# Even and odd batches as two streams half a round apart in a twelve-layer attention kernel

## The reference

```
x (8, 256, 128), cond (8, 128), context (8, 1601, 96)
 0 self  attention, 16 heads of 64, rotary     6 self  attention, 16 heads of 64
 1 cross attention, 16 heads of 64, rotary     7 cross attention, 16 heads of 64
 2 feed-forward (gelu)                         8 feed-forward (gated gelu)
 3 self  attention, 16 heads of 8              9 self  attention, 16 heads of 8, q and k normed
 4 cross attention, 16 heads of 8             10 cross attention, 16 heads of 8
 5 feed-forward (tanh gelu)                   11 feed-forward (gated silu)
attention: softmax(q k^T * dh^-0.5) v, projected; cross: the 1601 context rows are keys and values
```

## Time and profile before

| what | value |
|---|---|
| time, three runs | 6185.82, 6196.47 (median), 6211.56 us |
| profiled execution | 6242.82 us, of which the span of its instructions is 6241.0 us |
| mean granted TensorE clock in it | 0.898 of 2.4 GHz |
| busy: PE, DVE, ACT, POOL | 5692.5, 4360.4, 3383.1, 2505.9 us |
| PE's weight loads | 3349.0 us |
| DMA queue of the program | 124.68 MB, 8.5% of 16 engines' span |

### The profile page before, as it was taken

One profiled execution on the slowest core, in us unless ns is written; L12 is line 12 of the kernel. 1 busy time (PEld: TensorE's weight loads), 2 busy tenths in 40 slices (PEclk: granted clock), 3 DMA queues, 4 the chain that ended last, 5 costly groups with the idle time before them and its releaser, 6 DMA issues. The chain is left out here.

```text
span 6241.0 us, 170025 instructions
## 1 busy us (share of the span) xinstructions
PE 5692.5 (91%) x66584; PEld 3349.0 (54%) x66584; DVE 4360.4 (70%) x8986; ACT 3383.1 (54%) x7674; POOL 2505.9 (40%) x2223
## 2 busy tenths in 40 slices
PE   6999899988899989998889998999888998899988
PEld 4566346643556635664356653566435665356633
DVE  6886666656788666665788867666668886666664
ACT  3455565546544556554644556555564555655555
POOL 2566016730256501673026640277103663037700
PEclk9999699987899969998899987999779998699976
DMA  4000010000100001000010000100001000010000
GB/s 111 23 16 17 13 30 16 13 20 12 44 23 16 15 15 32 14 14 18 16 44 22 16 18 12 32 13 15 19 17 45 13 16 17 11 36 13 7 17 8
DMA packets 277771, 135.56 MB, mean 22 GB/s; under 512 B 151005, under 2 KB 266301, under 8 KB 276862
## 3 DMA queue, kind: packets, MB, share of 16 engines
q1 hardware_dynamic: 276990, 124.68, 8.5%
HBM read 101.90 MB, written 3.01 MB: 17 GB/s over the span
## 5 line engine op out<-in xcount | busy, mean ns | idle before, releaser
L2266 DVE TENSOR_REDUCE max_part<-ring 128x1 f32<-128x400 f32 (+2 forms) x4608 | 2418.6, 578 | 776.1 <-PE ring L1425 768.0
L1918 ACT ACTIVATE probs<-ring 128x512 f32<-128x512 f32 (+1 forms) x4096 | 2101.2, 572 | 1337.9 <-PE ring L1425 1312.4
L1401 POOL TENSOR_TENSOR weight_sum<-weight_sum,probs 128x512 f32<-128x512 f32 (+1 forms) x1408 | 1793.7, 1274 | 150.3 <-ACT probs L1918 11.5
L1425 PE MATMUL o_acc<-probs,region 128*32 128x256 f32 (+2 forms) x13312 | 1503.1, 441 | 47.2 <-ACT probs L1918 41.4
L1425 PEld LDWEIGHTS o_acc<-probs,region 128*32 128x32 f32 (+2 forms) x13312 | 617.2, 133 | 573.8 <-issue 262.4
L1401 POOL TENSOR_TENSOR weight_sum<-probs 128x512 f32<-128x512 f32 x256 | 332.1, 1297 | 1467.7 <-PE ring L1425 923.6
L1425 PE MATMUL ring<-qop,region 64*128 64x256 f16 x9984 | 833.1, 270 | 22.6 <-ACT shift_q L1763 16.7
L1763 ACT ACTIVATE region<-ring 65x128 f32<-65x128 f32 (+4 forms) x1232 | 560.9, 474 | 413.8 <-PE ring L1425 319.8
L1425 PE MATMUL ring<-nk,nq 32*128 32x400 f16 (+2 forms) x2560 | 601.9, 401 | 65.2 <-ACT probs L1918 51.1
L1425 PEld LDWEIGHTS ring<-qop,region 64*128 64x128 f16 x9984 | 522.2, 95 | 188.2 <-issue 92.1
L1425 PE MATMUL ring<-shift_q,shift_k 64*128 64x256 f16 (+1 forms) x3840 | 618.3, 270 | 0.0
(11 more groups left out here) (181 smaller groups left out, 6668.6 us busy)
## 6 DMA issues: line engine op xcount, KB each, us to landing
stage<-in_wide SPq DMA_DIRECT2D x448, 64.0 KB, 1.9
nk<-region SPq DMA_DIRECT2D x768, 25.0 KB
wo_stage<-in_wide SPq DMA_DIRECT2D x32, 512.0 KB, 4.0
stage<-in_wide SPq DMA_DIRECT2D x64, 128.0 KB, 2.5
v_stage<-in_wide SPq DMA_DIRECT2D x128, 64.0 KB, 1.9
ff_w<-in_ff_w SPq DMA_DIRECT2D x24, 256.0 KB, 3.3
stage<-kv_split SPq DMA_DIRECT2D x64, 96.0 KB, 2.1
v_stage<-kv_split SPq DMA_DIRECT2D x128, 48.0 KB, 1.7
```

The costliest lines, as they stand in the source:

```text
L1401: pool.tensor_tensor(total, before, probs[0:rows_, (un.chunk + k) % PROBS, :], ALU.add)\
L1425: return pe.matmul(out, lhs, rhs, start=start, stop=stop, skip_group_check=True)
L1918: act.activation(to, src, ACT.Exp, scale=t.scale).then_inc(exp_done.sem, 1)
L2266: dve.tensor_reduce(dst, src, AX.X, ALU.max).then_inc(*release(one))
```

## The change

- **Two streams.** `make_items` writes a new order. A *phase* has the self and cross attention of one kind of one stream and those of the other kind of the other stream: while the even batch is in its wide pair (0, 1 or 6, 7), the odd batch is in a narrow pair (9, 10 or 3, 4), and the other way round. There are 16 steps a stream and the odd stream runs one step behind, so there are 17 phases, the first without narrow and the last without wide units. In a phase come the narrow prelude, 8 wide self units, the prelude of the wide cross attention, 4 narrow self units, the prelude of the narrow cross attention, and then the cross units of both in the order `XXxXxXXxXx+XX` (X a wide, x a narrow one, + the prelude for what the narrow stream does next).
- **Buffers** go by the number of the unit in its own kind; maxima have four slots, two for each kind; narrow units have an output tile `attn_n` of their own; the narrow values (one set instead of two) and keys leave `region`, and the column of ones in the narrow values is set once at the start by POOL and not for each batch. `NK_SLOTS` goes from 3 to 2, `RING` from 4 to 5.
- **Rotary products.** The sine product goes to an SBUF buffer `raw_sin` as an instruction that can be ordered by itself, and its bank is free then; the add takes two SBUF operands and writes `raw`; ACT's high half reads `raw`, and so does DVE's low half. The number of instructions is the same.
- **Order of jobs.** A wide cross unit makes its keys first and its q last, so that keys need no tokens. All maxima follow. The transposed context moves to the prelude of sublayer 0, and its normed form to the start of the prelude of sublayer 1.
- **Weights.** The feed-forward weights are loaded ahead of each batch's layer and no longer once for two batches.
- In `Plan`, maxima of wide and narrow units are two queues instead of one. A maximum is still one product into one bank and one reduction.

```diff
-POOL_BANKS, RING, SLOTS, PROBS = 7, 4, 4, 8
+POOL_BANKS, RING, SLOTS, PROBS = 7, 5, 4, 8
-NK_SLOTS, VS_SLOTS = 3, 4
+NK_SLOTS, VS_SLOTS = 2, 4
...
-        out = op(0) + op(1) + [("low", 0, 0)] + op(2) + [("low", 1, 0)]
-        out += op(3) + [("low", 2, 0)] + maxima(0) + op(4) + [("low", 3, 0)] + maxima(1)
-        out += vals[0:1] + [("low", 4, 0)] + maxima(2) + vals[1:2] + maxima(3)
+        out = op(1) + op(2) + [("low", 1, 0)] + op(3) + [("low", 2, 0)] + vals[0:1]
+        out += op(4) + [("low", 3, 0)] + op(0) + [("low", 4, 0), ("low", 0, 0)]
+        out += maxima(0) + maxima(1) + vals[1:2] + maxima(2) + maxima(3)
...
+STAGES = ((0, 1), (3, 4), (6, 7), (9, 10))
+SHARED = "XXxXxXXxXx+XX"
+def make_items():
+    out = [("pre", 0, 0)]
+    steps = len(STAGES) * B // 2
...
+    for phase in range(steps + 1):
+        wide = narrow = None
+        for side in range(2):
+            i = phase - side
+            if 0 <= i < steps:
+                u, k = 2 * (i // len(STAGES)) + side, i % len(STAGES)
+                if k % 2:
+                    narrow = u, *STAGES[k], k
+                else:
+                    wide = u, *STAGES[k]
+        if narrow:
+            out.append(("pre", narrow[1], narrow[0]))
+        if wide:
+            for p in range(ATT[wide[1]].units):
+                unit(wide[1], wide[0], p)
+            out.append(("pre", wide[2], wide[0]))
+        if narrow:
+            for p in range(ATT[narrow[1]].units):
+                unit(narrow[1], narrow[0], p)
+            out.append(("pre", narrow[2], narrow[0]))
+        at = {"X": 0, "x": 0}
+        for what in SHARED:
+            if what == "X" and wide:
+                unit(wide[2], wide[0], at[what])
+            elif what == "x" and narrow:
+                unit(narrow[2], narrow[0], at[what])
...
     def low_parts(un, i):
...
+                    if t.rope:
+                        dve.tensor_tensor(operand(un, i, 1)[0], raw[:, raw_slot(un, i), 0:w], high, ALU.subtract)\
+                            .then_inc(rope_low.sem, 1)
+                        return
...
+                    if one[0] == "sin":
+                        dve.wait_ge(*full(made))
...
+                        dve.tensor_tensor(raw_sin[:, 0:w], v, rope_sin[:, a0:a0 + w], ALU.mult)\
+                            .then_inc(*release(made))
+                        return
...
-                    dve.tensor_tensor(v, v, rope_sin[:, a0:a0 + w], ALU.mult).then_inc(rope_step.sem, 1)
-                    dve.wait_ge(*taken(("job", n, j - 1)))
-                    dve.wait_ge(rope_step.sem, rope_step.at(n, 3 * i + 1))
-                    dve.tensor_tensor(v, v, products, ALU.add).then_inc(rope_step.sem, 2)
+                    for product in latest([("job", n, j - 1), made]):
+                        dve.wait_ge(*taken(product))
+                    dve.tensor_tensor(turned, turned, raw_sin[:, 0:w], ALU.add).then_inc(rope_step.sem, 1)
...
-            self.part("PE", "max", due, one, 0.1 if t.cross else 0.16, deps, 0.25)
+            self.part("PE", "wide max", due, one, 0.1 if t.cross else 0.16, deps, 0.25)
...
+            self.part("PE", "narrow max", due, one, 0.1 if t.cross else 0.16, deps, 0.25)
...
-                        if kind == "ffout" and u % 2 and (s, u) != (END, B - 1):
+                        if kind == "ffout" and (s, u) != (END, B - 1):
...
-                            load_hidden_weights((FFN[s - 1] + 1) % len(FFN))
+                            load_hidden_weights(next(hidden_at))
```

More of the change, by code:

```diff
@@ L169, in make_units @@
+ITEMS = make_items()
 def make_units():
     out, chunk, wide_at, narrow_at = [], 0, 0, 0
[L171 to L178, removed]
+    for kind, s, u, *rest in ITEMS:
+        if kind == "unit":
+            t = ATT[s]
+            out.append(Unit(len(out), t, u, *rest, chunk, wide_at, narrow_at))
+            chunk += t.chunks
+            wide_at += t.wide
+            narrow_at += not t.wide
@@ L179, in make_units @@
     return out
 UNITS = make_units()
+WIDES = [un for un in UNITS if un.t.wide]
+NARROWS = [un for un in UNITS if not un.t.wide]
+FIRST_UNIT = {(un.t.sub, un.u): un for un in UNITS if un.p == 0}
 LAST_UNIT = {(un.t.sub, un.u): un for un in UNITS if un.p == un.t.units - 1}
[L186 to L195, removed]
@@ L330, in make_order @@
         put(2.0 + 6.0 * i, "split", i)
-    clock, host = 0.0, free
-    for un in UNITS:
-        t, n = un.t, un.n
[L334 to L340, removed]
+    clock, units = 0.0, iter(UNITS)
+    for what, s, u, *_ in ITEMS:
+        if what == "pre":
+            place_prelude(s, u, clock if out else free)
+            continue
+        un = next(units)
+        t, n = un.t, un.n
+        if un.p == 0 and n:
+            clock = max(clock, begins[s, u] + (12.0 if t.wide else 14.0))
         for pair in range(t.pairs):
@@ L375, in holds @@
     kind, i, k = t.jobs[j]
-    if kind == "op" and not (t.rope and k == 0):
+    if kind == "op" and t.rope:
+        return "DVE", one if k == 0 else ("sin", one[1], j)
+    if kind == "op":
         return "DVE", ("job", one[1], t.jobs.index(("low", i, 0)))
@@ L500, in pre @@
             deps = [("POOL", ("scale", old.n))] if before.wide else [("ACT", here(m - 1))]
-            if before.wide and self.wide.index(old) >= 8:
+            if before.wide and self.wo:
                 deps.append(("SP", self.wo))
@@ L551, in wide_job @@
         if kind == "op":
-            deps = self.inputs(un) if j == 0 else []
+            deps = (self.context(un) if t.cross and i else self.tokens(un)) if k == 0 else []
             if j == 0 and at >= 2:
@@ L575, in wide_job @@
             old = [("PE", ("job", self.wide[at - 1].n, self.wide[at - 1].t.shift_job))] if at else []
[L576 removed]
+            self.part("DVE", "shift", due, one, 0.15, maxima + self.turned(un))
             self.part("ACT", "cols", due, ("cols", n), 0.2, [("DVE", one), *old])
@@ L614, in narrow_job @@
         old = self.narrow[un.narrow_at - 1] if un.narrow_at else None
-        self.part("DVE", "shift", due, one, 0.15, [*maxima, ("ACT", ("cols", n - 2))])
+        self.part("DVE", "shift", due, one, 0.15, maxima + self.turned(un))
         self.part("ACT", "cols", due, ("cols", n), 0.2,
```

345 lines of the change are left out of this document (192 added, 153 removed).

## The result

The changed kernel takes 6241.3 us (median of five runs, 6235.2 to 6257.5) against 6193.1 for the kernel before: ratio 1.008, 95% interval 1.0057 to 1.0103. It is slower by 0.8%, where 8% faster was forecast.

A forecast was written before the change was run, and what follows sets the result against it. Bound before the change: PE in wide cross attentions, DVE in sublayer 0, neither in narrow ones. A phases 2660, B phases 2536, phase 0 346 and the last phase 180 sum to 5722 us, scaled to 5680; range 5400 to 6120.

The forecast's parts named there:

- A phases: Seven mixed phases with the rotary pair (sublayers 0, 1): DVE 350 us, PE 341.5 us, forecast 380 us each.
- B phases: Eight mixed phases with the wide pair 6, 7: PE 301.3 us, DVE 232.9 us, forecast 317 us each.
- the last phase: Narrow work alone at the end, with the tail and some 9 us for missing cover: 180 us.
- phase 0: Wide work alone at the start, a lead of 28 us and 8 units of 25.5 us: 346 us.
- the budget of PE's work as busy time times granted clock: Estimate of PE's full-clock work per mixed phase: 341.5 us with the rotary pair, 301.3 us with pair 6, 7.
- the time the change can get at: Slow clock and mutual waits in narrow stages, and leads between stages; DVE's maxima waited 768 us for their products.
- The fill of 92 and 95%: How close mixed phases get to their bound: 92% for A phases, 95% for B phases.
- wrong altogether: Sign that the forecast fails: phases in which neither PE nor DVE passes 85%, the order itself making engines wait.
- The collision of two-operand reads: Rotary adds and low halves reading two SBUF operands contend with POOL: 40 us of DVE in an A phase, bounds 0 and 60.
- Rival (a): Rotary reads don't collide with POOL, so PE bounds A phases at 359 us: 5520 us in all; chance 0.14.
- Rival (b): Narrow maxima among wide work cost PE 0.2 us more each, 26 us a phase: 6000 us; chance 0.26.
- Rival (c): Narrow units in mixed stretches still bring PE to 1.2 GHz, 10 us for each of 60: 6275 us; chance 0.10.

The follow-up runs named there:

- The comparison of halves: Narrow cross units take maxima over two of four key chunks: changed kernel 5862.3 us (0.39 us saved per maximum), kernel before 6067.9 us (0.14 us).
- the hold of 4 us: Planner's constant STAY raised from 1.0 to 4.0, keeping PE longer on a tile shape: kernel before 6083.2 us (0.983), changed kernel 6155.0 us (0.9945).
- the two single edits: Changed kernel with the planner's STAY at 4.0 instead of 1.0, 6155.0 us; separately, changed kernel with rotary sums in PSUM again, 6147.6 us.
- both losses cut back: Changed kernel with rotary sums in PSUM and STAY at 4.0: 6018.2 us (0.968); with cross order XXxXxXxXXx+XX as well: 5993.5 us (0.966).
- the joint edits: Changed kernel with both rotary sums in PSUM again and STAY at 4.0: 6018.2 us, ratio 0.968, 246 us off.

## Why the prediction was wrong

The sum missed its span by 515 us (6237 against 5722). By its terms: A phases 413 on average instead of 380, 228 us; B phases 344 instead of 317, 216; the last phase 246 instead of 180, 66; phase 0 351 instead of 346, 5.

**The step that failed first is the budget of PE's work as busy time times granted clock,** together with the sentence that the slow clock and the waits of the narrow stages, the gap between 92 and 145 us a phase, are "the time the change can get at". I wrote that it might be "some us low". For a B phase the same measure gives 324.25 x 0.97 = 315 us now, against 301: the work doesn't keep its size when its neighbours change. The budget had no row for what lies *between* instructions, since the busy time of a modelled matmul swallows it. The 1610 added changes of shape, at 0.12 to 0.14 us, are some 13 to 15 us a phase, which is that difference. In an A phase it is 343 beside 3 and 4, where 341.5 was budgeted, and 355 beside 9 and 10. PE's busy total, forecast near 5300 us, is 5754. The comparison of halves shows the other side: the waits in narrow stages were not empty, maxima stood in them at 0.14 us each, and among the wide work they cost 0.39.

A number that could have been read beforehand points the same way. The planner adds 0.1 us for each change of shape (`dur += 0.1 * (tile_of(what) != tiled)`, in both kernels), and its own play-through (`PLAN.end`, which needs no chip) ends at 6251 us for the kernel before and at 6227 for the changed one: 0.4% faster, not 8%. It isn't exact, for it knows nothing of the collisions, and for the kernel before with the hold of 4 us it says 6226 where 6083 were measured. But a sum that promises 500 us more than the plan it rests on has something to explain.

**The fill of 92 and 95% was the second, and the larger.** On average a B phase reached 315/344 = 92%, not 95: of its 27 us too many, some 15 are the budget's and 12 the fill's. An A phase reached 343/391 = 88% by PE and 80% by DVE beside narrow 3 and 4, and 355/446 = 80% by PE and 79% by DVE beside 9 and 10. The latter comes near what the prediction named "wrong altogether", an order in which neither engine passes 85%, if PE is taken by its work at the full clock; by plain busy time PE has 92%. Two engines near their limit, each late for the other, may lose more than the worse of the two bounds says; the two single edits gave 84 and 93 us, and both together 246. Why a phase beside 9 and 10 takes 45 us more than one beside 3 and 4 was not sought: in the trace some 16 of them lie in the wide self units and some 22 in the narrow self ones, whose q and k are normed in sublayer 9.

**The collision of two-operand reads** was right in kind and over-sized: 40 us of DVE an A phase forecast, 185/8 = 23 measured; an instruction of a cross unit was to lose 0.42 us on average and lost 0.24 (add) and 0.32 (low half). I had set A as DVE's bound on its strength (350 of DVE against 341.5 of PE); DVE came to 313 and 350. With 23 us DVE's 333 would have been under PE's 341.5, and the sum's own rule would have given 341.5/0.95 = 359 an A phase. So this error hid 21 us a phase of the other two; that the sum missed by 515 us and not by some 660 is luck. Rival (a) is out. By the Trainium skill's rule ("SBUF — State Buffer", "Who interferes with whom") these reads contend with POOL's; the trace agrees, 894 ns against 571 for the same low half.

**Rival (b)** was the nearest. Its sign, PE busy near 100% in B phases of 340 us and over, came (95 to 96% of the phase, 97% of its mixed stretch), and so did its 344 us for a B phase. Its size is partly luck: it put 26 us a phase on the 128 narrow maxima alone, PE's work grew by 14, and the rest was fill. In all it had 321 us and a time of 6000. The Trainium skill's rule that a change of tiling mode drains TensorE ("TensorEngine Tiling (Array Packing)", "Key Properties") was cited there and not priced; the runs put 0.10 to 0.14 us on it. 1610 changes at 0.12 in the forecast's sum would have brought it some 200 us nearer, and left it 300 short.

**Rival (c)** ended on the right side by another road. The clock didn't dip at each narrow cross unit: the mixed stretch of B holds 1.00. It fell to 0.87 in an A phase. Dense changes of shape don't explain that: between phase 0 and the last, the stretches at 0.50 (724 us) have 0.7 changes a us by the trace, those at 1.00 have 1.1. What brought it down there is open. **The last phase** runs at a mean clock of 0.61, with nothing beside it: 66 us over my 180, which I had priced as half of two batches that ran after each other and could cover each other's gaps.

Right were: no narrow dips of the page's kind, though the clock didn't stay at 0.95 in all slices; DVE's waits for products down (768 to 530 us), free loads and key buffers (no such wait stands among the long ones), and B's DVE at 227 to 235, 233 being budgeted.

What stays open is, first, the larger part of the miss: with both losses cut back the kernel stands at a ratio of 0.966 to 0.968, where 0.917 was forecast. Then how the 246 us of the joint edits split between PE, DVE and the order that the planner found with the other hold: that order is a new one each time, and only the short products were measured in an unchanged order. The other edits of the change (two key buffers instead of three, `RING` 5, the order of jobs, the weights of each batch loaded anew) were not taken back one by one.

## What to carry to other kernels

Before interleaving two kinds of work on one engine, count what the interleaving adds between them, here changes of tile shape in PE's list, and price one change by inserting a tiny product of the other shape into the kernel as it is. Count the changes that it adds in the list or in the trace, not by the number of products. If a planner writes the order, read its own end time first. And don't take idle time of a slow stage for room: remove half of the work you mean to hide and see what it costs where it stands now. Try the scheduling constant on the kernel before as well; here it gave 1.7% without any restructuring, and the streams are worth another 1.7% only on top of it.

## What the runs showed of the hardware

- A change between 64-row and 32-row products costs PE 0.12 us averaged over a kernel (410 us for 3356), 0.14 us in a settled PE-bound unit (3.97 us for 28) and 0.10 to 0.11 us in a program of matmuls alone at the full clock; with column-tiled products among them, 0.11 to 0.13 us at 1.2 GHz.
- PE that alternates shapes every two products shows 100% busy and, after a first stretch at 1.00, a granted clock of 0.50 (1.2 GHz). The sign for it in a profile is the weight loads' share: 14.09 of 40.90 us there, 11.31 of 13.20 in uniform work.
- A DVE `TENSOR_TENSOR` of 400 f32 columns with both operands in SBUF took 819 to 894 ns on average in a kernel with POOL busy for 41% of the time, with one in PSUM 571 to 583 ns. The adds that met no POOL instruction took 569 ns on average, those almost wholly beside one 999.
